# The first half of the closing norm and FFN moved into the last slots of a gated delta-rule kernel, its inverse root on GpSimd

## The reference

```python
x = x + 0.5 * ffn(layernorm(x))      # "FFN 0"
x = x + attn(layernorm(x))           # gated delta rule, 16 heads of 128
x = x + 0.5 * ffn(layernorm(x))      # "FFN 1", same weights

# layernorm: (x - mean) / sqrt(var + 1e-5), over the 256 features, no weights
# ffn: x@W_base + b_base + (x@A_s)@B_s + sum over e of (x@A_r[e] * w[e]) @ B_r[e]
#      w = softmax(x@W_router + b_router) with only its 2 largest of 6 kept; rank R = 16
# attn: q, k, v = projections; q and k normalised; causal depthwise convolution of 4 taps, SiLU;
#       state S = S*exp(g); S += beta * k (v - k S);  o = q S, token after token;
#       out = (rmsnorm(o) * sigmoid(gate)) @ Wo
```

## Time and profile before

| | us |
|---|---|
| median of 3 executions | 1018.1 |
| the three | 1025.29, 1018.1, 1017.93 |
| the profiled execution, its own time | 1025.84 |
| its span, first to last instruction | 1023.7 |
| PE busy in the span | 957.6 |
| DVE, ACT, POOL busy | 812.7, 708.9, 72.2 |
| mean granted TensorE clock | 0.975 of full |

### The profile page before, as it was taken

How to read it: one execution, slowest core, us unless ns; L and a number is a source line. 1 busy time by engine, 2 the same in 40 slices (tenths; PEclk the granted TensorE clock), 3 DMA queues, 4 the chain that set the end, 5 groups by cost and what they waited for, 6 DMA issues and landing times.

```text
span 1023.7 us, 34567 instructions
## 1 busy us (share of the span) xinstructions
PE 957.6 (94%) x15274; PEld 729.2 (71%) x15274; DVE 812.7 (79%) x1707; ACT 708.9 (69%) x1558; POOL 72.2 (7%) x176
## 2 busy tenths in 40 slices
PE   4898699999999999999999999999999998999966
PEld 4534367777787777777777777778777777788855
DVE  5576689888888888898888888898888887667724
ACT  2376668778877787778778787887787875545431
POOL 7000000000000000000000000000000000000000
PEclk9898799999999999999999999999999997999989
DMA  6100111100000010200001112000000000000001
GB/s 160 50 1 13 29 30 31 40 13 12 13 2 3 30 31 30 78 6 12 12 3 30 31 31 71 14 13 12 13 12 13 12 9 6 13 13 3 3 1 42
DMA packets 29033, 24.14 MB, mean 24 GB/s; under 512 B 4626, under 2 KB 24276, under 8 KB 28884
## 3 DMA queue, kind: packets, MB, share of 16 engines
q1 hardware_dynamic: 28884, 21.94, 7.7%
HBM read 20.82 MB, written 1.11 MB: 21 GB/s over the span
## 4 chain that ended last, share of the span: by engine, by line
PE 88%; DVE 5%; ACT 5%; issue 1%; DMA 1%; SPq 0%; POOLq 0%; POOL 0%; DVEq 0%; ACTq 0%
PE psum L800 17%; PE psum L823 10%; PE psum L864 8%; PE psum L846 8%; PE psum L855 7%; PE psum L923 6%; PE psum L810 3%; PE psum L806 3%; PE psum L901 3%; PE psum L895 3%; PE psum L888 3%; PE psum L881 3%; PE psum L815 2%; PE psum L874 2%; PE psum L830 2%; PE psum L912 2%
## 5 line engine op out<-in xcount | busy, mean ns | idle before, releaser
L800 PE MATMUL psum<-hT,gw 128*128 128x512 f32 x384 | 188.2, 616 | 1.7 <-DVE pairs L1250 0.9
L823 PEld LDWEIGHTS psum<-kq,ks 128*64 128x64 f32 x3072 | 106.4, 138 | 75.0 <-issue 45.3
L1206 DVE SCALAR_TENSOR_TENSOR qkv<-pad,chan,qkv 128x512 f32<-128x512 f32 x192 | 134.3, 739 | 0.3
L823 PE MATMUL psum<-kq,ks 128*64 128x64 f32 x3072 | 124.1, 227 | 8.8 <-DVE tot L1244 4.5
L1232 DVE TENSOR_TENSOR kq<-kq,tot 128x512 f32<-128x512 f32 x160 | 109.6, 685 | 25.0 <-PE psum L823 25.0
L800 PEld LDWEIGHTS psum<-hT,gw 128*128 128x128 f32 x384 | 68.7, 196 | 63.8 <-issue 61.7
L846 PE MATMUL psum<-tmat,pairs 64*64 64x32 f32 x2560 | 102.8, 220 | 5.0 <-ACT tmat L538 4.6
L846 PEld LDWEIGHTS psum<-tmat,pairs 64*64 64x64 f32 x2560 | 89.9, 136 | 21.3 <-issue 11.8
L1250 DVE COPY_PREDICATED pairs<-masks,psum 128x256 f32<-128x256 uint8 x192 | 101.0, 526 | 4.7 <-PE psum L823 4.6
L864 PE MATMUL psum<-pairs,fmat 64*64 64x32 f32 x2560 | 102.5, 220 | 0.9 <-DVE fmat L1217 0.9
L864 PEld LDWEIGHTS psum<-pairs,fmat 64*64 64x64 f32 x2560 | 90.7, 136 | 9.3 <-issue 6.0
(11 more groups left out here) (154 smaller groups left out, 1719.9 us busy)
## 6 DMA issues: line engine op xcount, KB each, us to landing
bb<-beta_rows SPq DMA_DIRECT2D x32, 256.0 KB, 3.3
gw<-in_L_attn_Wq SPq DMA_DIRECT2D x16, 128.0 KB, 2.3
gw<-in_L_attn_Wk SPq DMA_DIRECT2D x16, 128.0 KB, 2.4
gw<-in_L_attn_Wv SPq DMA_DIRECT2D x16, 128.0 KB, 2.3
gwo<-in_L_attn_Wo SPq DMA_DIRECT2D x4, 512.0 KB, 5.8
x<-in_L_attn_hidden_states SPq DMA_DIRECT2D x4, 256.0 KB, 4.6
gfb<-in_L_attn_Wfb SPq DMA_DIRECT2D x16, 64.0 KB, 2.1
ggb<-in_L_attn_Wgb SPq DMA_DIRECT2D x4, 256.0 KB, 4.8
```

What stands on the lines that cost most here:

```text
L800: last = eng.matmul(two(bank[to]), gw[:, t, kt, hh * D:(hh + 1) * D], two(hT[:, kt])[:, :, h * PW:(h + 1) * PW], start=(kt == 0), stop=(kt ...
L823: last = eng.matmul(o[rows(b), :, u], ks[:, p, tokens(b, u)], half(kq[:, p, :, tokens(b, u)], h, 1), start=True, stop=True)
L1206: last = eng.scalar_tensor_tensor(out=piece(t, i), in0=src, scalar=tap_weight(t, tap, i), in1=piece(t, i), op0=ALU.mult, op1=ALU.add)
```

## The change

It puts the first half's norm and the start of its FFN into the slots of the last items:

- the centred rows of that half go to `early_hn`, a view of `rr`, and the squares' by-product to `early_junk`, a view of `sq`; both buffers are used by the early stages of items and idle from slot 28 on;
- DVE centres that half between slots 29 and 30;
- ACT squares it between slots 30 and 31, with the mean taken by the instruction's scale (1/16 before the square), and does no logarithm and exponential for it;
- POOL adds epsilon and takes the power -1/2 between its slots 31 and 32 (new constant `eps_ln`, one more memset at the start);
- the load of the logarithm and exponential tables stays between slots 32 and 33 of ACT;
- `ln_move(2, 0)` goes into slot 33 on ACT (behind `osq`) and DVE (behind `ssq`), and `ln_turned(2, 0)` and `ffn_low(1, 0)` into slot 33 of PE, ahead of the wait for `turn_output`;
- on DVE, the first half's `ffn_logits` and `ffn_gates` now stand ahead of the last `add_output`, and its `ffn_add` stands between `ln_scale(2, 1)` and `ln_move(2, 1)`;
- on PE, the first half's `ffn_turn`, `ffn_base` and `ffn_experts` now stand ahead of `ln_turn(2, 1)`;
- on ACT, the first half's `ffn_exponent` and `ffn_move` stand ahead of `ln_scales(2, 1)`.

```diff
+        eps_ln = sb("eps_ln", [P, HALF])
+        early_hn = rr[:, :, :].rearrange("p a (c d) -> p (a c) d", d=HID)
+        early_junk = sq[:, :, :].rearrange("p a (c d) -> p (a c) d", d=HID)
+        def normed(f, k):
+            if f == 2 and k == 0:
+                return early_hn
+            return hn[:, tiles_of(k)]
@@ gpsimd
+            eng.memset(eps_ln[:, :], EPS_LN)
+            def early_inverse():
+                eng.wait_ge(early_squared, 1)
+                eng.tensor_tensor(st[:, 3, tiles_of(0)], st[:, 2, tiles_of(0)], eps_ln[:, :], ALU.add).then_inc(pool_chain, 1)
+                eng.wait_ge(pool_chain, 10)
+                eng.tensor_tensor(st[:, 4, tiles_of(0)], st[:, 3, tiles_of(0)], mhalf[:, 0:HALF], ALU.pow).then_inc(ln_rstd, 1)
-            for t in range(-5, NCK + 2):
+            for t in range(-5, NCK):
+                slot(t)
+            early_inverse()
+            for t in range(NCK, NCK + 2):
                 slot(t)
@@ scalar, slot(t)
                     eng.activation(osq, bank[O_BANK][:, :], ACT.Square).then_inc(osq_ready, 1)
+                    if t == NCK + 1:
+                        ln_move(2, 0)
@@ scalar
-            for t in range(-5, NCK + 1):
+            for t in range(-5, NCK - 1):
+                slot(t)
+            eng.wait_ge(ln_centred, 5)
+            for c in range(HALF):
+                last = eng.activation(early_junk[:, c], early_hn[:, c], ACT.Square, scale=float(HID) ** -0.5,
+                                      accum_out=st[:, 2, c:c + 1])
+            last.then_inc(early_squared, 1)
+            for t in range(NCK - 1, NCK + 1):
                 slot(t)
             table(LN_EXP)
-            ln_scales(2, 0)
             slot(NCK + 1)
-            table(LN_EXP)
-            ln_move(2, 0)
+            ffn_exponent(1, 0)
+            ffn_move(1, 0)
             ln_scales(2, 1)
-            ffn_exponent(1, 0)
             ln_move(2, 1)
-            ffn_move(1, 0)
             ffn_exponent(1, 1)
             ffn_move(1, 1)
@@ tensor, slot(t)
                 if 0 <= n2 < NCK:
+                    if t == NCK + 1:
+                        ln_turned(2, 0)
+                        ffn_low(1, 0)
                     after(on_ready, n2 + 1)
                     turn_output().then_inc(ot_done, 1)
@@ tensor
             ln_turn(2, 0)
             slot(NCK + 1)
-            ln_turned(2, 0)
-            ffn_low(1, 0)
+            ffn_turn(1, 0)
             ffn_base(1, 0)
-            eng.wait_ge(x_added, NCK)
+            ffn_experts(1, 0)
             ln_turn(2, 1)
-            ffn_turn(1, 0)
             ln_turned(2, 1)
             ffn_low(1, 1)
-            ffn_experts(1, 0)
             ffn_base(1, 1)
             ffn_turn(1, 1)
             ffn_experts(1, 1)
@@ vector, slot(t)
                     eng.tensor_reduce(ssq[:, 0], gd(osq), AX.X, ALU.add).then_inc(ssq_ready, 1)
+                    if t == NCK + 1:
+                        ln_move(2, 0)
...
-                    after(wo_done, n2 + 1)
-                    add_output(n2).then_inc(x_added, 1)
+                    if n2 < NCK - 1:
+                        after(wo_done, n2 + 1)
+                        add_output(n2).then_inc(x_added, 1)
@@ vector
-            for t in range(-5, NCK):
+            for t in range(-5, NCK - 2):
                 slot(t)
-            eng.wait_ge(vs_ready, NCK)
             eng.wait_ge(x_added, NCK - HALF)
             ln_centre(2, 0)
-            slot(NCK)
+            for t in range(NCK - 2, NCK + 1):
+                slot(t)
             ln_scale(2, 0)
-            ln_move(2, 0)
             slot(NCK + 1)
+            ffn_logits(1, 0)
+            ffn_gates(1, 0)
+            eng.wait_ge(wo_done, NCK)
+            add_output(NCK - 1).then_inc(x_added, 1)
             eng.wait_ge(x_added, NCK)
             ln_centre(2, 1)
-            ffn_logits(1, 0)
             ln_scale(2, 1)
-            ffn_gates(1, 0)
+            ffn_add(1, 0)
             ln_move(2, 1)
             ffn_logits(1, 1)
             ffn_gates(1, 1)
-            ffn_add(1, 0)
             ffn_add(1, 1)
```

More of the change, by code:

```diff
@@ L172, in build @@
         low_done, low_copied, beta_done, beta_exp, beta_ready, beta_turned, beta_copied = sems("low_done low_copied beta_done beta_exp beta_ready beta_turned beta_copied")
-        pool_free, = sems("pool_free")
+        pool_free, early_squared = sems("pool_free early_squared")
         wos_ready, rms_chain = sems("wos_ready rms_chain")
@@ L713, in ln_turn @@
                         last = eng.transpose(bank[TURN_BANKS[f][i][kt]][:, c * P:(c + 1) * P],
-                                             hn[:, i * HALF + c, kt * P:(kt + 1) * P], ident[:, :])
+                                             normed(f, i)[:, c, kt * P:(kt + 1) * P], ident[:, :])
                     last.then_inc(ln_tr, 1)
@@ L1104, in ln_centre @@
                 link(eng.tensor_scalar(st[:, 1, i], st[:, 0, i], 1.0 / HID, None, ALU.mult))
-                eng.tensor_tensor(hn[:, i], x[:, i, :], spread(st[:, 1, i], HID), ALU.subtract).then_inc(ln_centred, 1)
+                eng.tensor_tensor(normed(f, k), x[:, i, :], spread(st[:, 1, i], HID), ALU.subtract).then_inc(ln_centred, 1)
             def ln_scale(f, k):
@@ L1109, in ln_scale @@
                 eng.wait_ge(ln_rstd, 2 * f + k + 1)
-                eng.tensor_tensor(hn[:, i], hn[:, i], spread(st[:, 4, i], HID), ALU.mult).then_inc(ln_ready, 1)
+                eng.tensor_tensor(normed(f, k), normed(f, k), spread(st[:, 4, i], HID), ALU.mult).then_inc(ln_ready, 1)
             def ln_move(f, i):
```

## The result

| | before | after |
|---|---|---|
| median, us | 1019.14 (6 executions, 1017.93 to 1025.29) | 1009.7 (6, 1008.54 to 1013.73) |
| profiled execution, its own time | 1025.84 | 1013.73 |
| its span | 1023.7 | 1011.9 |
| mean granted clock | 0.975 | 0.982 |

The ratio is 0.9916, with a 95% interval of 0.9894 to 0.9939: faster by 0.8%, 8.6 us of the 1019.14. The forecast was 1008.0 in a range of 1004.5 to 1014.5. It was made from a median of 1018.1, the one of the three executions known then; with six, the median before is 1.0 higher, and that is 1.0 of the 1.7 us by which the forecast is off.

What follows compares the result with a forecast made beforehand. PE, busy for 94% of the span, bounds the slots, so only the tail behind slot 31 can give; -5.6 us up to ln_turn(2, 1) and -4.5 behind it make -10.1, taking 1018.1 to 1008.0 us, range 1004.5 to 1014.5.

Steps and rivals of the forecast that it cites:

- The slots cost nothing: Norm work put on DVE, ACT and POOL in slots 29 to 32 adds 0 us; slots stay 22.84 long.
- Rival 2: The slots pay: squares delay inverse_y(5) by up to 1.7 us, ln_centre slot 30 by 0.9; 1010.6 us, chance 0.09.
- Part 1, the wait: Between slots 32 and 33, only the table load remains on ACT, so inverse_y(5) starts 2.17 us earlier.
- rival 3: The table switch costs the documentation page's price: ACT stands 1.4 us longer behind the load; 1009.4 to 1011 us, chance 0.04.
- Part 1, the clock: Behind inverse_y(5), PE runs at full clock: project_output of item 30 saves 1.20 us, inverse_turned(5) 0.37.
- Rival 1: The clock falls again behind PE's shorter tail waits: 1.8 us before queries_new ends, more later; 1011 with two, chance 0.17.
- Part 1, two batches at -0.14 each: Two batches behind inverse_turned(5) shorten from 1.02 and 1.04 us to a full slot's 0.88 and 0.90.
- Part 2: From the end of item 31's queries_new to ln_turn(2, 1): 15.5 us instead of 17.0.
- Part 3: From ln_turn(2, 1) to ffn_turn(1, 1): 7.7 us instead of 12.2, so -4.5; the 8.37 behind it unchanged.
- The sum: Gains of 5.6 us up to ln_turn(2, 1) and 4.5 behind it: -10.1, a span of 1013.6 for 1023.7.
- Rival 5: An unseen wait ties inverse_y(5) or the second half to the old time; one part gained, 1012 to 1014, chance 0.08.
- rival 4: PE stays at 1.2 GHz from 975 to the end, costing 13.3 us: 1021 us, slower than before, chance 0.02.

Runs made afterwards that it cites:

- e1: The changed kernel run again unaltered; median 1009.46 us, ratio to before 0.9904, tail (ssq of slot 32 to span end) 47.3 us.
- e2: The changed kernel with ACT's table load moved into slot 32 behind scale_output; median 1007.56 us, ratio to before 0.9872, tail 46.9 us.
- e3: The changed kernel with three idle matmuls filling PE's two waits at the end of slot 32; median 1010.68 us, tail 47.7 us.
- e6: The changed kernel with the first half's norm still early but the tail's order taken from the kernel before; ratio to before 0.9958, tail 53.2 us.
- e9: The kernel of e2 run again unaltered; times 1007.09 to 1016.7 us, ratio to before 0.9899, tail 46.9 us.
- e10: The kernel of e9 with PE's two waits for DVE in slot 27 filled with idle matmuls (the fill); median 1008.88 us, tail 46.85 us.
- e11: The kernel of e9 with ffn_add(1, 0) behind ln_move(2, 1) on DVE instead of ahead of it; tail 46.84 us.
- e12: The changed kernel with the table load early, PE's slot 27 waits filled and ffn_add(1, 0) later; median 1008.15 us, ratio to before 0.9875.
- e8: The changed kernel with the last add_output and the second half's centre ahead of the first half's gates on DVE; median 1016.15 us, tail 56.0 us.
- e4: The changed kernel with the first half's inverse root back on ACT instead of POOL, squares still early; tail 49.1 us.
- e5: The kernel before run again unaltered; span 1014.5 us, tail 56.7 us.
- e7: The changed kernel with the new tail order, but the first half's norm where it was before; ratio to before 0.9949, tail 51.8 us.

## Why the prediction was right

- **The slots cost nothing: right.** 22.85 us each, and squares, centre and POOL as worked out. Rival 2 is out.
- **Part 1, the wait: right, to 0.01.** `inverse_y(5)` starts 7.93 behind the slot's `ssq`, 10.09 before: -2.16 for the -2.17 of the sum. The load shows its 1.28 and the copy 0.02 behind, as in the earlier trace rows; rival 3 is out.
- **Part 1, the clock: this is the step that failed in the profiled execution.** "So I take full clock" was wrong there: `project_output` took 3.15 as before. It was right in e1, e2, e3, e6 and e9 to e12. Behind waits of 0.79 and 0.38 the clock held in e1 and e6 and fell in the profile after and in e8. It fell in all four with longer ones (e4, e5, e7 and the kernel before), and it held in the six with only the 0.79 or with both filled. That is the pattern of a clock that falls by the waits, but 2 falls in 4 against 0 in 6 can still be chance. Rival 1 named it, at 1.8; it costs 1.6. The reading behind the step was too kind: "waits of PE up to 0.6 long" leaves out the 0.95 and 1.95 of slot 27, behind which the clock had fallen in the very profile that the prediction was read from, and a wait of 0.88 in each of slots 28 to 31, behind which it fell in none of the fourteen profiles.
- **Part 1, two batches at -0.14 each: this term is not there.** In e1, at full clock, `queries_state` starts at 976.99 and `solve` at 978.01: still 1.02. The 0.88 and 0.90 of a slot are ahead of a batch of smaller matmuls (64x32). The 1.02 was no sign of a low clock. This is 0.3 of my sum.
- **Part 2: right.** From the end of `queries_new` (979.52) to `ln_turn(2, 1)` (994.89) it is 15.4 for the 15.5 worked out, 17.0 before, with the gates ahead of the addition as what is late.
- **Part 3: 0.5 short, and the end another 0.5.** hT comes 2.03 behind `ln_turn` and not 1.75, the gates take 4.12 and not 4.03: 8.2 for 7.7. The 1.75 is just the transposes (1.06) and the copy (0.69); the addition and the copy of the same sentence give 1.99 by themselves. With the addition out of the way (e11) it is still 1.96, so its place is 0.07 of the miss, and the other 0.2 are handovers that the sum leaves out, 0.14 from the copy to PE above all. From `ffn_turn(1, 1)` on it is 8.83 and not the unchanged 8.37: the batch now starts behind a wait and takes 0.71 on the chain where it took 0.45 right behind `ffn_base`, and from the last addition to the end of the span it is 5.42 for 5.22, the end that e4 and e7 do not have.
- The sum: a tail of 46.2 forecast, 47.3 where the clock holds, 48.9 in the profile. In the time, it is 1008.0 against 1009.7 (and 1009.46 in e1). The ratio says 0.8%, on the side of "within 1%", to which I had given 0.58; with a forecast on the border, the side is no merit of the sum. Rival 5 is out, since both parts of the gain came (e6, e7), and so is rival 4: the clock is 1.00 behind 976.
- **The frame.** I took the 7.7 us between the profiled execution and the median as a fixed difference. That execution had the long slot 28 (5.9 us) and a first `ssq` in the later part of its range (161.66); the median's execution has no trace, so that these two are the 7.7 is likely and not shown. Since the change works in the tail alone, taking its gain off the median stood all the same. This scatter also widens every interval here: the before's 6 executions alone span 7.4 us.

## What to carry to other kernels

Before two spans are subtracted, lay a ruler along both: an instruction that comes once an item tells in one table which microseconds belong to the change. Work off the path is free only up to the place where the next engine's queue runs dry, and here the best witness for that was the trace of the same three instructions at another place of the kernel. When a chain is reordered in the tail, the in-order queues decide more than the waits: the same gates delay the last addition by 1.1 us when they stand ahead of it, and the tail by 7 when they stand behind it, 4 of them by the order and 3 by the clock that falls in the long wait.

## What was not expected of the hardware

- The clock behind one and the same wait is not one and the same. Behind waits of 0.95 and 1.95 us in slot 27 (0.95 and 1.96 in the profile after) slot 28 is short in eight of the twelve profiles without the fill and long in four (before, e1, e6, e9), at 5.9 us each. In all four the mean clock is 0.51 to 0.53 over 14 us behind the second wait. No single profile of a kernel shows whether it has this. The start of the attention varies by 5.1 us besides, and the times alone do not tell the two apart.
- A batch of 16 matmuls of 128x128 (`queries_state`) or 64x128 (`solve`) takes 0.88 and 0.90 on the chain where a batch of 64x32 follows, and 1.02 and 1.05 where its like or a wait follows, all at 2.4 GHz.
